# Cross-attention with its last key tiles in units of their own, and idle products on TensorE in a fused decoder layer

## What is computed

```python
x = x + attn(layernorm(x))                  # retention-like attention with a causal mask, 16 heads of 8
x = x + xattn(layernorm(x), ctx_1024)       # cross-attention over 1601 keys
x = x + ffn(layernorm(x))                   # 2 layers of local attention (8 heads of 64) with a gated feed-forward
```

```python
q = (query @ Wq.T).reshape(B, 256, 16, 8) * 8 ** -0.5
k = (key @ Wk.T).reshape(B, 1601, 16, 8)
v = (value @ Wv.T).reshape(B, 1601, 16, 8)
scores = sigmoid(einsum('blhd,bshd->bhls', q, k))    # a sigmoid of each score, no softmax
o = einsum('bhls,bshd->blhd', scores, v).reshape(B, 256, 128)
return o @ Wo.T
```

## Time and profile before

| | us |
|---|---|
| median of 3 runs (1788.62 to 1791.8) | 1788.67 |
| the profiled execution's own time | 1783.75 |
| its span, first to last instruction | 1781.9 |
| TensorE busy (95%) | 1685.1 |
| ScalarE busy (80%) | 1424.7 |
| VectorE busy (57%) | 1019.3 |
| GpSimd busy (26%) | 454.7 |
| mean granted clock of TensorE | 0.990 |

### The profile page before, as it was taken

One profiled execution on the slowest core, in us unless ns is written; L12 is line 12 of the kernel. 1 busy time (PEld: TensorE's weight loads), 2 busy tenths in 40 slices (PEclk: granted clock), 3 DMA queues, 4 the chain that ended last, 5 costly groups with the idle time before them and its releaser, 6 DMA issues. The chain is left out here.

```text
span 1781.9 us, 66416 instructions
## 1 busy us (share of the span) xinstructions
PE 1685.1 (95%) x28128; PEld 1019.0 (57%) x28128; DVE 1019.3 (57%) x3178; ACT 1424.7 (80%) x2649; POOL 454.7 (26%) x387
## 2 busy tenths in 40 slices
PE   7998899999999999999999978999999979999998
PEld 4785555555555555555555435666663346666643
DVE  4566543333443333344333058999984489999954
ACT  4444899999999999999999957888884368898852
POOL 1115000000000000000000027777730177877500
PEclk9999999999999999999999989999999999999999
DMA  2000311111111111111110030111110001111100
GB/s 63 1 0 25 125 50 50 64 51 45 64 65 50 50 51 49 61 64 55 54 36 32 3 113 20 34 36 24 32 34 15 0 19 32 27 35 32 31 18 36
DMA packets 47421, 73.33 MB, mean 41 GB/s; under 512 B 8400, under 2 KB 38224, under 8 KB 47184
## 3 DMA queue, kind: packets, MB, share of 16 engines
q1 hardware_dynamic: 47184, 69.85, 12.7%
HBM read 21.08 MB, written 2.10 MB: 13 GB/s over the span
## 5 line engine op out<-in xcount | busy, mean ns | idle before, releaser
L690 ACT ACTIVATE x_probs<-x_pss 128x1024 f32<-128x1024 f32 x832 | 806.4, 1021 | 35.3 <-PE x_pss L611 4.0
L625 PE MATMUL x_acc<-x_probs,x_v 128*32 128x256 f32 x6656 | 435.8, 379 | 0.0
L611 PE MATMUL x_pss<-x_qx,x_kx 32*128 32x256 bf16 x9984 | 347.0, 269 | 6.9 <-ACT x_probs L690 2.1
L611 PEld LDWEIGHTS x_pss<-x_qx,x_kx 32*128 32x128 bf16 x9984 | 221.8, 93 | 189.9 <-ACT x_probs L690 171.2
L625 PEld LDWEIGHTS x_acc<-x_probs,x_v 128*32 128x32 f32 x6656 | 207.9, 110 | 82.9 <-issue 5.3
L737 DVE COPY x_vnext<-x_psp 128x128 f32<-128x128 f32 (+1 forms) x197 | 58.2, 295 | 314.3 <-PE x_psp L589 313.8
L1520 ACT ACTIVATE l_prob<-l_neg_sim,l_neg_top 128x128 f32<-128x128 f32 x512 | 198.6, 396 | 6.0 <-DVE l_neg_top L1334 6.0
L951 POOL TENSOR_TENSOR l_turned_half<-l_raw,l_tabB 128x512 f32<-128x512 f32 x128 | 186.3, 1477 | 49.2 <-ACT l_raw L1479 46.7
L666 POOL COPY x_zq<-zT 128x256 f32<-128x256 f32 x15 | 6.0, 403 | 746.3 <-PE x_psp L596 680.6
L961 POOL TENSOR_TENSOR l_direct<-l_direct,l_turned_half 128x1024 f32<-128x1024 f32 x64 | 151.5, 2367 | 0.0
L1334 DVE CUSTOM_DVE_ANT_0 l_neg_sim<-l_pss,w_window,l_inv_norm 128x128 f32<-128x128 f32 x512 | 149.1, 348 | 3.5 <-issue 2.8
(11 more groups left out here) (206 smaller groups left out, 2622.0 us busy)
## 6 DMA issues: line engine op xcount, KB each, us to landing
x_kx<-x_kp SPq DMA_DIRECT2D x96, 208.0 KB, 2.3
x_cT<-in_context SPq DMA_DIRECT2D x16, 832.0 KB, 4.6
x_qx<-x_qp SPq DMA_DIRECT2D x48, 192.0 KB, 2.3
l_vmid<-l_vt SPq DMA_DIRECT2D x64, 128.0 KB, 2.3
xT<-in_x SPq DMA_DIRECT2D x8, 256.0 KB, 6.3
shifted<-zT SPq DMA_DIRECT2D x32, 64.0 KB, 2.0
hs<-zT SPq DMA_DIRECT2D x32, 64.0 KB, 2.0
out_x<-xT SPq DMA_DIRECT2D x8, 256.0 KB, 2.0
```

Source lines behind the costliest of these rows:

```text
L611: ins = pe.matmul(pss[bank(k, 2 * p + r // 2)][:, r % 2, e, :], kx[par][rows, g, j * P:(j + 1) * P], qx[par][rows, g, a * S:(a + 1) * S], ...
L625: ins = pe.matmul(acc[32 * r:32 * r + 32, 0:S], v[:, j, g, r, :], probs[SLOT[p]][r // 2][:, r % 2, e, :], start=(u == 0), stop=(u == UNITS ...
L690: act.activation(probs[SLOT[p]][y][:, :, :, :], pss[bank(k, 2 * p + y)][:, :, :, :], ACT.Sigmoid, scale=HD ** -0.5).then_inc(weighed, 1)
```

## The change

The keys of a batch are grouped anew. The 12 full tiles of the four groups are 48 units in 24 pairs, as before. The 64 keys that follow are taken for two groups in one unit: the upper 64 partitions of the score buffer hold one group's, the lower 64 another's, so one pair (`TAILS`) holds the tails of all four groups, with 48 score matmuls of 32x64. The last key (`LONE`) has a unit of its own: GpSimd spreads the key's column over a block (`klone`), 12 matmuls of 128x32 give the scores of all 16 heads, ScalarE does one sigmoid of 128x256, and the mix is 4 products with `vlone` in place of 8. A batch then has 25 pairs and a single unit, with 51 sigmoids; as 51 is a multiple of 3, the buffers no longer rotate from batch to batch. The value projection has one row of values more (`MT + 1`), which the last value piece takes along; VectorE sets two tail copies and one last-key copy more per batch (`set_tails`). The context is padded with copies of its last key instead of zeros, and two small tables are loaded.

Besides, `idle_products` issues products that nobody reads: 5 ahead of the second variances of each norm, 11 for 8 between the widenings and 4 behind them; 4 ahead of retention's first projection, 11 behind its first turn, 5 at its end; 6, 5 and 3 in the lead-in of cross-attention; 6 at the start of each local layer, and 4 to 8 at five places of its turns -1 and 0. The core of the diff:

```diff
-ST = (CTX + P - 1) // P
-CTXP = ST * P
+MT = CTX // P
+TAIL = CTX - MT * P - 1
+LASTKEY = MT * P + TAIL
+assert TAIL == 64 and MT % 2 == 0
+CTXP = (MT + 1) * P
+VT = MT + 2
 KCH = CTXP // HG
-VCH = [(0, 4), (4, 7), (7, 10), (10, 13)]
+VCH = [(0, 4), (4, 8), (8, 12), (12, 14)]
...
+def idle_products(pe, ones_mean, to, times):
+    for _ in range(times):
+        pe.matmul(to, ones_mean[:, :], ones_mean[:, :], start=True, stop=True)
...
+            idle_products(pe, ones_mean, var[1][:, 0:P], 5)
             variances(1)
             widen(0)
-            keep_warm(WARM)
+            idle_products(pe, ones_mean, mean[0][:, 0:P], WARM)
             widen(1)
+            idle_products(pe, ones_mean, mean[0][:, 0:P], 4)
...
+            def first_turn_or_turn(n, u):
+                turn(n, u)
+                if isinstance(n, int) and n == 0:
+                    idle(11)
+            idle(4)
             project(0, 0)
             project(1, 1)
-            turns(pe, turn)
+            turns(pe, first_turn_or_turn)
+            idle(5)
...
-    PAIRS = HG * ST // 2
-    UNITS = HG * ST
+    MAIN = HG * MT // 2
+    PAIRS = MAIN + 2
+    TAILS, LONE = MAIN, MAIN + 1
+    WEIGHTS = 2 * PAIRS - 1
+    SETS = HG + 2 + 1
...
+        def bank(h):
+            return h % 3
...
+        def tokens_of(j, rows):
+            if j < MT:
+                return [(lo, j * P + lo) for lo in range(0, P, rows)]
+            if j == MT:
+                return [(lo, j * P + lo % TAIL) for lo in range(0, P, rows)]
+            return [(lo, LASTKEY) for lo in range(0, P, rows)]
...
+                for i in ((j,) if j < MT else (MT, MT + 1)):
+                    for lo, at in tokens_of(i, 32):
+                        ins = pe.matmul(psp[lo:lo + 32, (i - j) * D:(i - j + 1) * D], cT[par][:, at:at + 32],
+                                        w["wv"][:, :], start=True, stop=True)
...
+                if p == LONE:
+                    score_lone(n, par)
+                    return
+                if n > 0 or p > 0:
+                    pe.wait_ge(weighed, n * WEIGHTS + 2 * p - 1)
                 for e in range(2):
-                    g, j = divmod(2 * p + e, ST)
+                    if p < TAILS:
+                        g, j = divmod(2 * p + e, MT)
+                        parts = [(0, P, g, j * P)]
+                    else:
+                        parts = [(lo, TAIL, 2 * e + lo // TAIL, MT * P) for lo in (0, TAIL)]
                     for a in range(PARTS):
-                        for r in range(HL):
-                            rows = slice(32 * r, 32 * r + 32)
-                            ins = pe.matmul(pss[bank(k, 2 * p + r // 2)][:, r % 2, e, :], kx[par][rows, g, j * P:(j + 1) * P],
-                                            qx[par][rows, g, a * S:(a + 1) * S], start=(a == 0), stop=(a == PARTS - 1))
+                        for lo, size, g, key in parts:
+                            for r in range(HL):
+                                rows = slice(32 * r, 32 * r + 32)
+                                ins = pe.matmul(pss[bank(2 * p + r // 2)][lo:lo + size, r % 2, e, :],
+                                                kx[par][rows, g, key:key + size],
+                                                qx[par][rows, g, a * S:(a + 1) * S], start=(a == 0), stop=(a == PARTS - 1))
...
+            def score_lone(n, par):
+                pe.wait_ge(lone_ready, n + 1)
+                pe.wait_ge(weighed, n * WEIGHTS + 2 * LONE - 2)
+                for a in range(PARTS):
+                    for g in range(HG):
+                        ins = pe.matmul(pss[bank(2 * LONE)][32 * g:32 * g + 32, 0, 0, :], klone[par][:, g, :],
+                                        qx[par][:, g, a * S:(a + 1) * S], start=(a == 0), stop=(a == PARTS - 1))
+                ins.then_inc(scored, 1)
...
+                pe.wait_ge(weighed, n * WEIGHTS + (2 * p + 2 if p < LONE else WEIGHTS))
+                if p >= TAILS:
+                    pe.wait_ge(v_set, n * SETS + HG + 2 + (p - TAILS))
+                for e in range(2 if p < LONE else 1):
+                    g, j = divmod(2 * p + e, MT)
+                    if p < TAILS and j == 0:
+                        pe.wait_ge(v_set, n * SETS + g + 1)
                     for r in range(HL):
-                        ins = pe.matmul(acc[32 * r:32 * r + 32, 0:S], v[:, j, g, r, :],
-                                        probs[SLOT[p]][r // 2][:, r % 2, e, :], start=(u == 0), stop=(u == UNITS - 1))
+                        if p < TAILS:
+                            values = v[:, j, g, r, :]
+                        elif p == TAILS:
+                            values = vtail[:, (e * HL + r) * 32:(e * HL + r + 1) * 32]
+                        else:
+                            values = vlone[:, r, :, :].rearrange("p g d -> p (g d)")
+                        ins = pe.matmul(acc[32 * r:32 * r + 32, 0:S], values,
+                                        probs[SLOT[p]][r // 2 if p < LONE else 0][:, r % 2 if p < LONE else 0, e, :],
+                                        start=(p == 0 and e == 0), stop=(p == LONE))
...
             project_first()
-            score(0, 0, 0, 0, 0)
+            idle(5)
+            score(0, 0, 0, 0)
+            idle(3)
             turns(pe, turn)
...
+            def lone_keys(n, par, half):
+                pool.wait_ge(stacked[par], (half + 1) * PACKED)
+                if n >= 2:
+                    pool.wait_ge(scored, (n - 1) * PAIRS)
+                pool.tensor_tensor(klone[par][:, :, 0:HL], kx[par][:, :, LASTKEY:LASTKEY + 1].broadcast_to([P, HG, HL]),
+                                   w["block"][:, :].unsqueeze(1).broadcast_to([P, HG, HL]), ALU.mult).then_inc(lone_ready, 1)
+            lone_keys(0, 0, 0)
...
+                    if p == LONE:
+                        act.activation(probs[SLOT[p]][0][:, 0, 0, :], pss[bank(2 * p)][:, 0, 0, :], ACT.Sigmoid,
                                        scale=HD ** -0.5).then_inc(weighed, 1)
+                    else:
+                        for y in range(2):
+                            act.activation(probs[SLOT[p]][y][:, :, :, :], pss[bank(2 * p + y)][:, :, :, :], ACT.Sigmoid,
+                                           scale=HD ** -0.5).then_inc(weighed, 1)
...
+            def set_tails(n, copied):
+                dve.wait_ge(freed, copied)
+                if n > 0:
+                    dve.wait_ge(mixed, (n - 1) * PAIRS + TAILS + 1)
+                for s in range(2):
+                    rows = slice(TAIL * s, TAIL * s + TAIL)
+                    to = vtail[rows, :].rearrange("p (w x) -> p w x", w=2)[:, :, 0:HL * 32]
+                    dve.tensor_copy(to.rearrange("p w (h x) -> p w h x", h=HL)[:, :, :, HD * s:HD * (s + 1)],
+                                    vnext[rows, MT, :].rearrange("p (w s h d) -> p w s h d", w=2, s=2, h=HL)[:, :, s, :, :]
+                                    ).then_inc(v_set, 1)
+                if n > 0:
+                    dve.wait_ge(mixed, n * PAIRS)
+                dve.tensor_tensor(vlone[:, :, :, :], vnext[:, MT + 1, :].rearrange("p (g h d) -> p h g d", g=HG, h=HL),
+                                  w["corner"][:, :, :, :], ALU.mult).then_inc(v_set, 1)
...
                 turn_over(later(x, -1), 1, 0)
+                idle(x, -1, 4)
                 project_q(later(x, 2), 1)
                 value(later(x, -1), 0)
                 turn_over(later(x, -1), 1, 1, x)
+                idle(x, 0, 4)
                 score(x, 1)
                 value(later(x, -1), 1)
+                idle(x, -1, 5)
                 flip_q(later(x, 1), 0)
                 turn_over(x, 0, 0)
                 project_k(later(x, 2), 1)
                 project_out(later(x, -1))
+                idle(x, -1, 5)
+                idle(x, 0, 8)
...
+            idle_products(pe, ones_mean, pso[:, 0, :], 6)
             turns(pe, turn, 4)
```

More of the change, by code:

```diff
@@ L137, in widen @@
                               start=True, stop=True).then_inc(spread, 1)
-            def keep_warm(times):
-                for _ in range(times):
-                    pe.matmul(mean[0][:, 0:P], ones_mean[:, :], ones_mean[:, :], start=True, stop=True)
             if project is not None:
@@ L218, in _, with retention @@
             guess(1)
-def retention(nc, zT, w, vb):
+def retention(nc, zT, w, vb, ones_mean):
     CK = 64
@@ L560, in project_first @@
                 for c in range(V0):
+                    if c == 2:
+                        idle(6)
                     if c >= 2:
@@ L627, in mix, with turn @@
                 ins.then_inc(mixed, 1)
-            def turn(n, par, half, k, last=False):
+            def turn(n, par, half, last=False):
                 first = isinstance(n, int) and n == 0
@@ L1227, in chunk, with idle @@
                 widen(n, 2)
+            def idle(x, n, times):
+                if isinstance(x[0], int) and x[0] == n:
+                    idle_products(pe, ones_mean, pso[:, 0, :], times)
             assert HC == 3
```

(12 more changed lines are left out.)

72 lines of the change are left out of this document (36 added, 36 removed).

## The result

The changed kernel takes 1778.34 us as the median of 4 executions (1775.2 to 1779.67), the kernel before 1788.64; the ratio is 0.9941, interval 0.9922 to 0.9959. The forecast was 1779.5. The profiled execution took 1779.67 us with a span of 1777.9, against 1783.75 and 1781.9 before: only 4.1 us apart, while the medians are 10.3 apart. That gap is itself one of the results.

The account below looks back on a forecast made before the run. TensorE's own work was taken to bound cross-attention in 15 batches, with ScalarE's loop close behind and setting batch 15. Cross-attention -6.2 and idle products -3.0 sum to -9.2 us, from 1788.67 to 1779.5 us, range 1769 to 1790.

Parts of the forecast that it names:

- The fixed 0.98 us: Cross-attention, TensorE's time from mix to next scores: the same behind value and key pieces, so TensorE sets the pace.
- Rival 2: Cross-attention: ScalarE sets the pace after all, 26 us saved there, 1759.5 us in all; chance 0.06.
- last-key scores and the mix ahead: Cross-attention batch: 0.34 us of scores for 0.76, and 0.09 off the mix ahead without the shape change: -0.51 us.
- turn into the next batch: Turn crossing into the next cross-attention batch: its scores find their sigmoids long done, 1.98 us for 2.06: -0.07.
- Batch 15: Last cross-attention batch, set by ScalarE's loop: a pair turn and a second sigmoid go: -1.5 us, between -1.0 and -2.0.
- Rivals 3 and 4: Tails' halves in turn, 1788.8 us (0.16 together with Rival 5); also with weight loads bared, 1805 (0.11 with smaller forms).
- the far bound: Tails' scores in cross-attention: halves run in turn, six more score groups, +0.67 us per batch.
- Rival 5: Cross-attention: last-key scores wait for GpSimd's block or tail copies for VectorE, 1787 us; 0.16 together with rival 3.
- The loop entry of retention: 11 idle products (2.8 us) meet TensorE's idle 2.83 us at retention's loop entry: +0.3 us, range 0 to 2.8.
- 1.54 us each: Six idle products straight before each local layer's first projection: cost 1.54 us per layer, uncovered in layer 2.
- the -1.4 that I set against it: Local layer 1's start: the slow clock costs 1.4 us there, which the six idle products would give back.
- Rival 1: Half-clock stretches only move and idle products still cost their place, +1.9 us for them, 1784.4 in all; chance 0.17.

Follow-up runs that it names:

- the keys alone: Changed kernel without its added idle products, leaving the new key grouping and the 8 idle products per norm of before: 1782.69 us, ratio 0.996.
- no local product: Changed kernel without any idle product in the local layers, neither the six at the start nor the 26 in the turns: 1774.72 us, ratio 0.9919.
- The best version: Changed kernel without the six idle products at each local layer's start and with both layers sharing cosine, sine, window and identity tiles: 1764.87 us, ratio 0.9875.

## Why the prediction was right, and where only its total was

**What bounds cross-attention: right.** The fixed 0.98 us was the argument, and the run with short key pieces shows both halves of it: TensorE's work is the turn, ScalarE's loop of 1.965 lies right behind. Rival 2 falls.

**The batch: right, every term within 0.04 us.** Forecast -0.31 us, measured 52.44 to 52.02, -0.42:

| term | forecast | measured |
|---|---|---|
| tails' scores | +0.05 | +0.03 (0.76 to 0.79) |
| second value row | +0.24 | +0.23 (0.24 to 0.47) |
| last-key scores and the mix ahead | -0.51 | -0.43 and -0.12 |
| last-key mix | -0.02 | -0.02 |
| turn into the next batch | -0.07 | -0.07 |

Another -0.03 is the piece behind the last-key scores, which reaches its mix in 0.21 us for 0.24. The shape change was put at 0.09 and is 0.12 here (mix to last-key scores 0.86 for 0.98): the scores after a mix start later when the tile shape changes. The Trainium skill's TensorEngine Tiling (Array Packing), Key Properties, says that a change of tiling mode drains the engine; the trace agrees, with these 0.12 us. Batch 15 came to -1.2 for -1.5, in its range. Rivals 3 and 4 fall by the trace, and by the run with the halves in turn their price falls too: the +0.67 us that I had set as the far bound, on the assumption that two halves issued in turn can't overlap, is 0.10. Rival 5 falls: nothing waits before the last-key scores. The whole regrouping, forecast at -6.2 us, is -7.7 by the stages of the two profiles and -5.6 by the medians of the keys alone.

**The idle products: total right, terms wrong by cancelling errors.** By medians they are -8.0 for a forecast of -2.35 in norms, retention and lead-in, -6.3 for -2.3 in the local turns, and +10.0 for +1.6 at the starts: -4.3 in all for -3.0. That the total held is luck. Three steps failed.

1. *I counted the half-clock stretches of one execution.* That execution had a mean clock of 0.990 and took 1783.75; 41 timed executions of the same kernel have a median of 0.988. An estimate from the two: 0.988 of 1786 us is 43 us at half clock, where the profile has 34, so some 4.5 us of time, which is what the median lies above the profiled execution. Where the others hold these stretches no profile of this kernel shows. The profile of the keys alone, whose retention is unchanged, has 6.8 us at retention's loop entry and 6.8 in the first turns of the batches; products there would have that to give back. This is also why the profiled executions are 4.1 us apart and the medians 10.3.
2. *The loop entry of retention: +0.3 forecast, nothing paid.* The 22 matmuls take 2.72 us where TensorE stood idle 2.83, and the turn got 0.1 us shorter (row below). At retention's start, forecast at 0, the warm clock gave 1.2 back.
3. *The starts of the local layers.* The step "1.54 us each" held only for layer 2 (1.41). In layer 1 it is 2.7, since TensorE stands idle for 3.7 us ahead of them and the clock is down (2.1 to 2.7 us in the five profiles that have them); the -1.4 that I set against it for a warm lead-in (23.20 us before) did not come with the products (25.83 us to the first mask), only without them (21.53, in two profiles of four). And in layer 2 they bring the wait of 2.3 to 3.1 us for "issue", in four of five profiles with a stretch at 0.50 behind it. Of the 5.2 us that layer 2's six cost, 1.4 is their place and 2.3 to 3.1 that wait; the rest fits one such stretch. Of layer 1's 4.7, up to 2.7 is their place; the rest stays open. The row of step 2, of the changed kernel:

```profile
39.03 2.72 PE L51 MATMUL r_sc<-ones_mean 128*128 128x128 f32 x22
```

**Norm 3: forecast 0, measured +1.4.** The forecast looked only at products ahead of the norm. What sets its end is SP's queue, with two long issues of 1.55 and 1.46 us in this profile, so products within norm 3 had next to nothing to win there.

**The signs I named.** Batch period, tails' scores, last-key scores, the mix ahead of them and VectorE's first key cut came as written; "none at norm 2 or at the start of cross-attention" too. "Fewer than five stretches at 0.50" was wrong: there are six, one of double length, among them new ones behind the 1.82 us wait of each feed-forward (1369 and 1734). That wait is in every profile; such a stretch followed it in feed-forward 1 in four of the thirteen profiles and in feed-forward 2 in seven, and costs 1.5 to 2 us when it comes. It comes with and without the six, but only in the nine profiles of kernels with products within the local turns; the four without (both of before, the keys alone, no local product) have none. So it may well be the change's, part of what those products give back; no run separates this from chance. "Layer's first projection 1.5 us later": right in layer 2 only. Rival 1 (the slow stretches only move) is out for the first half of the kernel; for the local starts it was half right, and the feed-forward stretches fit it.

## What to carry to other kernels

Idle products belong where a measured gap ends in another engine's work, never straight ahead of the work that the path begins with: those in gaps were worth 14 us together, the twelve in front of two layers cost 10. Where a half-clock stretch falls differs between executions, so the clock's price is read from the timed executions' mean clock, not from the stretches of one profile. And before a stage is sped up, look which queue issues its loads: norm 3's end came 0.69 us after the DMA queue's last issue in nearly every profile, and sharing four loads brought some 2 to 3.5 us.

## What the runs showed of the hardware

- The same program's time follows its mean granted clock closely: 41 executions of the kernel before took 1783.2 to 1784.2 us at 0.990, 1790.5 to 1794.4 at 0.985, and 1794.4 at 0.981. The best version reached 0.999.
- Twelve more matmul records in layer 2, whose results nobody reads, brought a wait of 2.3 to 3.1 us that the profile gives to nothing but "issue", 38 us or more behind them, whether they stood at the block's start or behind turn -1's key projection: in all five profiles with them, in none of the eight without. The same twelve in layer 1 brought none there.
- Issuing a load took SP 0.47 us apiece, but single ones took up to 2.31 us, and their number and place differed between executions.
- The 48 score products of 32x64, issued one column half after the other, took 0.89 us, for 0.79 with the halves by turns; twelve groups of four at the 0.11 us of a group would be 1.3.
